# Adding the output projection to x straight from its bank, without ScalarE's copy

## The chip, the cores and the metric

The kernel runs on one core of a Trainium2 chip. The metric is the time on the device in microseconds (us): the median of several executions. The profile is one further execution, recorded by the hardware. TensorE (PE) multiplies matrices into eight banks of accumulators; VectorE (DVE) and ScalarE (ACT) can read these banks; GpSimd (POOL) here masks, divides and issues gathers and scatters; SyncE (SP) issues most of the transfers (DMA).

## The reference

One layer of a transformer over x of shape (8, 512, 256) in float32: attention, and then a mixture of experts.

```python
x = x + attn(layernorm(x))
# attn: qkv = x @ W_qkv + b_qkv; 16 heads of width 16, causal softmax of q k^T / 4
#       out = softmax(...) @ v;  return out @ W_out + b_out      (256 x 256)
x = x + ffn(layernorm(x))
# ffn: residual = x; xn = layernorm(x) * gamma + beta
#      probs = softmax(xn @ gate_w), 8 experts, the best 2 of each row with their shares
#      h = gelu(xn @ w1[e] + b1[e])  (256 -> 1024);  out_e = h @ w2[e] + b2[e]
#      return sum of the two out_e by share + residual
```

The change concerns `out @ W_out + b_out` and the `x +` in front of it.

## The kernel before

The kernel has three stages. In the **first** (about 140 us) the eight batches of 512 rows are normalised, turned and multiplied by `W_qkv`; q, k and v go to DRAM. The **attention** stage (to about 535 us) has 32 units, four heads of one batch each, so four units a batch. A unit is five combos; in each, TensorE computes scores in transposed form in two banks (`scores_T`, L657), whose exponentials ScalarE takes (L906, L903), and for a unit further on the scores in plain form (L629, masks L642), whose row maxima VectorE takes (`maxima`, L1236 to L1242). GpSimd masks the exponentials (L1699), TensorE weighs v by them (`weigh`, L701), ScalarE copies the result out (L926), and transfers through DRAM lay it out by heads; VectorE inverts the sums (L1249), GpSimd multiplies (`divide`, L1676). The **third** stage gathers rows by expert in 39 tiles and runs both layers of the experts (L776, L794), with gelu (L995) and the split of hidden values into two float16 parts (L1529, L1531), and scatters the results. Its first tiles run while the last batch is still on its way through the steps below.

Between attention and experts each batch b goes through a chain of its own, which is woven into the attention of the next batch:

- `load_again(b)` (SyncE, L1889) loads x of the batch again into `rows`, 512 KB. It waits until the batch before has given `rows` up.
- `out_proj(b, half)` (TensorE, L715 for the products in float32, L716 for the bias) makes 2 x 128 rows of the projection, 512 columns wide, in one bank.
- `copy_out(b, half)` (ScalarE, L959) copies the bank into `turned` in SBUF and frees the bank. `turned` also holds the turned rows of the batch before until `gate(b - 1)` (TensorE, L732) has read them.
- `add_out(b, half)` (VectorE, L1259) adds `turned` and `rows` into `x2`. It waits for the load of x (`x_again`) and until `x2` of the batch before has been stored (`rows_out`, L1977).
- then moments (L1266), variance, roots, shifts, scaling of rows on ScalarE (L935, L941), gamma and beta, the split of rows in two halves (L949, L1078), the turn of rows (L723, L931), the gate's product (L732) and its copy (`copy_gate`, L965), the choice of two experts and the places of rows.

**The order of the work is written down in advance.** `at(tick, stage, n)` puts each step at a tick of one table; every engine takes its own steps from the table in the order of ticks. A unit has 48 ticks and a batch 192. Ticks are places in an order and no times: an engine takes its next step when its semaphores allow, and never leaves one out. For batch b the base is the end of its four units plus 8 ticks (78 for the last batch); in that count the projection halves stand at 175 and 187, the copies at 181 and 193, the additions at 193 and 205, and the moments from 196 on. The gate of the batch before comes at 180 and its copy at 185.

**Banks.** Scores in transposed form and all the small products (top turns, projections, turned rows, gates, counts) take turns in banks 4, 5 and 6 in the order of the table; bank n's next user waits for the step that took out what the last one left (`TAKEN_BY`). For small products that was always ScalarE, counted by the semaphore `act_freed`; for scores it is the exponential (`exped`). So in batches 1 to 5 the order of uses is projection half 0, gate, then the two score halves of the first combo of a unit; the second of these has the bank that the projection had. In batch 0, without a gate, it is the projection's own second half.

Of the kernel before, what the change touches and what calls it, by code (L numbers as in the profile page):

```python
# [6 lines left out]
ALU = mybir.AluOpType  # L7
# [54 lines left out]
def build(nc, t):  # L62
# [54 lines left out]
    with ctx:  # L117
# [199 lines left out]
        def at(tick, stage, n):  # L317
            table_of.setdefault(tick, []).append((stage, n))
# [59 lines left out]
        for b in range(B):  # L378
# [3 lines left out]
            for half in range(2):  # L382
                at(base + 175 + 12 * half, "out_proj", (b, half))
                at(base + 181 + 12 * half, "copy_out", (b, half))
                at(base + 193 + 12 * half, "add_out", (b, half))
            for tt in range(TT):
# [52 lines left out]
        for j in range(-1, TILES):  # L439
# [10 lines left out]
            if j >= 0:  # L450
# [3 lines left out]
                if j + 2 < TILES:  # L454
# [8 lines left out]
        BANKS_A_UNIT = len(E_USES)  # L463
        TAKEN_BY = {"top_turn": "top_copy", "out_proj": "copy_out", "turn_x": "copy_x", "gate": "copy_gate",
                    "count": "copy_count"}
        uses, side, freed = [], {}, {"act_freed": 0, "exped": 0}
        for stage, n in timetable:
            if stage == "combo":
                for i in range(2):
                    freed["exped"] += 1  # L470
                    uses.append((("combo", n), ("combo", n), "exped", freed["exped"]))
            elif stage in TAKEN_BY:
                freed["act_freed"] += 1
# [356 lines left out]
        def scalar(act):  # L830
# [123 lines left out]

            def copy_out(b, half):
                w.wait_ge(sem("side_made"), side_made("out_proj", (b, half)))
                if b > 0:
                    w.wait_ge(sem("side_made"), side_made("gate", b - 1))
                act.copy(turned[:, half, :], side_bank("out_proj", (b, half))).then_inc(sem("act_freed"), 1)  # L959

            def copy_gate(b):
# [61 lines left out]
            for stage, n in timetable:  # L1023
# [6 lines left out]
                elif stage == "copy_o":  # L1030
                    copy_o(n)
                elif stage == "copy_out":
                    copy_out(*n)
                elif stage == "copy_gate":
# [37 lines left out]
        def vector(v):  # L1072
# [178 lines left out]
            def add_out(b, half):  # L1251
                w.wait_ge(sem("x_again"), 16 * (b + 1))
                w.wait_ge(*side_out("out_proj", (b, half)))
                if b > 0:
                    w.wait_ge(sem("rows_out"), 16 * b)
                else:
                    w.wait_ge(sem("v_store1"), 16 * (B // 2))
                own_x = slice(2 * half, 2 * half + 2)
                v.tensor_tensor(x2[:, own_x, :], turned[:, half, :].rearrange("p (s d) -> p s d", s=2), rows[:, own_x, :],  # L1259
                                ALU.add).then_inc(sem("out_added"), 1)  # L1260

# [756 lines left out]
```

## Time and profile before

| | |
|---|---|
| median of three runs | 972.66 us (967.0 to 973.46) |
| the profiled execution | 973.39 us, its span 971.6 us |
| TensorE busy | 844.1 us (87%), mean granted clock 0.927 of full speed |
| VectorE busy | 702.2 us (72%) |
| ScalarE busy | 572.8 us (59%) |
| GpSimd busy | 468.5 us (48%) |

The span runs from the first to the last instruction of the profiled execution. A row of the timeline has the start, the busy time, the engine, the line, the operation, what it writes and reads and how many instructions are merged in it; in square brackets stands how long the engine sat idle before it and what ended that. An idle time "issue" is one for which the profile shows no other engine or transfer as releaser. The lines of the program that load, store and add are seen under the names of the memory they lie in: `arena` and `weights` are SBUF, `banks` the accumulators. "SPq" is the issue of a transfer by SyncE; the transfer lands later. The granted clock of TensorE has two levels, 2.4 GHz (1.00) and 1.2 GHz (0.50); a mean between them is a mix over time.

### The profile page before, as it was taken

How to read it: one execution, taken by the hardware profiler on the slowest of the kernel's cores; microseconds unless marked ns; L12 is line 12 of the kernel's file. 1: busy time of each engine (PE TensorE's matmuls, PEld its weight loads, DVE VectorE, ACT ScalarE, POOL GpSimd, SP SyncE). 2: the span in 40 equal slices, each digit the busy share in tenths (PEclk: the TensorE clock that was granted, in tenths of full speed). 3: DMA queues.
4: the chain of work that ended last, by engine and by line, in shares of the span. 5: the costliest groups of instructions: out<-in, count | busy, mean ns of one | idle time of the engine just before them, and what ended most of it. 6: DMA issues, size and time to landing. Idle time of an engine off the chain costs nothing.

```text
span 971.6 us, 21008 instructions
## 1 busy us (share of the span) xinstructions
PE 844.1 (87%) x6760; PEld 555.8 (57%) x6760; DVE 702.2 (72%) x1566; ACT 572.8 (59%) x1048; POOL 468.5 (48%) x575
## 2 busy tenths in 40 slices
PE   4899988677797878787888797989989999999996
PEld 2555433233243424242434695869868888888875
DVE  6677888668669798979885585756756766656664
ACT  1767476546868787869776372545534445445453
POOL 4100033233535757657566556566566554554441
PEclk9999988779888979898997898989999999999998
DMA  8888667746767767576726884435535444444331
GB/s 202 253 274 270 235 190 195 194 113 170 206 195 204 184 188 198 163 200 179 203 75 208 169 145 69 58 79 98 79 55 79 79 78 73 76 76 83 52 73 23
DMA packets 185048, 139.40 MB, mean 143 GB/s; under 512 B 98065, under 2 KB 167569, under 8 KB 184817
## 3 DMA queue, kind: packets, MB, share of 16 engines
q1 hardware_dynamic: 153444, 95.16, 38.4%
q0 software_dynamic: 15776, 18.95, 12.3%
q10 hardware_dynamic: 15724, 23.95, 7.7%
q8 instruction: 61, 1.00, 0.4%
q14 instruction: 43, 0.34, 0.1%
HBM read 83.63 MB, written 44.80 MB: 132 GB/s over the span
## 4 chain that ended last, share of the span: by engine, by line
PE 54%; DVE 16%; DMA 13%; issue 5%; SPq 5%; ACT 3%; another core or an unknown queue 1%; POOL 1%; POOLq 0%; ACTq 0%; DVEq 0%
PE banks L776 18%; PE banks L794 18%; PE banks L598 5%; DMA weighed_values<-arena 3%; PE banks L715 3%; DVE arena L1239 3%; DMA inverse_sums<-arena 3%; DVE weights L1401 2%; PE banks L701 2%; PE banks L588 2%; PE banks L657 2%; SPq L1817 2%; DVE arena L1241 1%; SPq L1815 1%; DMA out<-arena 1%
## 5 line engine op out<-in xcount | busy, mean ns | idle before, releaser
L995 ACT ACTIVATE arena<-banks,arena 128x256 f32<-128x256 f32 (+1 forms) x312 | 152.4, 541 | 206.4 <-issue 95.7
L776 PE MATMUL banks<-arena,weights 128*128 128x256 f16 (+1 forms) x1872 | 210.9, 268 | 16.3 <-issue 15.7
L794 PE MATMUL banks<-weights,arena 128*128 x1704 | 198.2, 275 | 5.4 <-DVE arena L1531 3.1
L776 PEld LDWEIGHTS banks<-arena,weights 128*128 x1872 | 175.8, 99 | 45.5 <-issue 20.7
L1738 POOL DMA_INDIRECT out<-arena x71 | 117.0, 1648 | 159.1 <-DVE arena L1542 108.0
L794 PEld LDWEIGHTS banks<-weights,arena 128*128 128x128 f16 x1704 | 166.0, 99 | 31.1 <-issue 9.0
L657 PE MATMUL banks<-arena 64*128 64x128 f16 (+3 forms) x512 | 118.9, 330 | 32.8 <-ACT arena L931 9.3
L1529 DVE TENSOR_SCALAR arena<-arena 128x512 f16<-128x512 f32 (+1 forms) x156 | 76.9, 493 | 75.5 <-ACT arena L995 63.7
L629 PE MATMUL banks<-arena 62*128 62x384 f16 (+3 forms) x512 | 93.9, 326 | 32.5 <-DVE arena L1242 11.1
L1531 DVE SCALAR_TENSOR_TENSOR arena<-arena 128x512 f16<-128x512 f32 (+1 forms) x156 | 110.1, 706 | 5.6
L657 PEld LDWEIGHTS banks<-arena 64*128 64x128 f16 x512 | 38.0, 99 | 118.7 <-issue 36.3
L1239 DVE TENSOR_REDUCE arena<-banks 128x2 f32<-128x1024 f32 x64 | 77.8, 1216 | 31.0 <-PE banks L642 28.5
L906 ACT ACTIVATE arena<-banks,arena 128x512 f32<-128x512 f32 x128 | 81.3, 685 | 21.1 <-PE banks L657 20.7
L906 ACT ACTIVATE weights<-banks,arena 128x512 f32<-128x512 f32 x128 | 80.5, 685 | 12.4 <-PE banks L657 11.0
L1714 POOL DMA_INDIRECT arena<-token_rows,arena x71 | 75.2, 1060 | 21.1 <-issue 18.3
L1685 POOL DMA_INDIRECT slot_tokens<-arena x64 | 68.5, 1070 | 25.5 <-issue 16.3
L1241 DVE TENSOR_REDUCE arena<-banks 128x2 f32<-128x768 f32 x64 | 60.7, 949 | 22.7 <-PE banks L642 16.6
L1699 POOL TENSOR_SCALAR_AFFINE_SELECT weights<-weights 128x512 f32<-128x512 f32 (+1 forms) x80 | 45.2, 582 | 65.5 <-ACT weights L906 62.5
L1542 DVE SCALAR_TENSOR_TENSOR arena<-banks,arena 128x256 f32<-128x256 f32 x71 | 31.4, 480 | 62.1 <-PE banks L794 44.5
L1699 POOL TENSOR_SCALAR_AFFINE_SELECT arena<-arena 128x512 f32<-128x512 f32 (+1 forms) x80 | 49.1, 631 | 33.6 <-ACT arena L906 31.5
L701 PE MATMUL banks<-arena 128*32 128x256 f32 (+3 forms) x512 | 57.7, 530 | 4.8 <-ACT arena L926 2.4
L701 PE MATMUL banks<-weights 128*32 128x256 f32 (+3 forms) x512 | 57.7, 527 | 3.6 <-DMA weights<-v_rows 2.9
(199 smaller groups left out, 1259.9 us busy)
## 6 DMA issues: line engine op xcount, KB each, us to landing
weights<-in_L_ffn_w ACTq DMA_DIRECT2D x16, 1024.0 KB, 7.6
arena<-in_L_ffn_w SPq DMA_DIRECT2D x32, 512.0 KB
qk_parts<-weights SPq DMA_DIRECT2D x64, 128.0 KB
arena<-qk_parts SPq DMA_DIRECT2D x128, 64.0 KB, 3.5
weighed_values<-arena SPq DMA_DIRECT2D x32, 256.0 KB
token_rows<-arena SPq DMA_DIRECT2D x12, 512.0 KB, 4.3
arena<-qk_parts SPq DMA_DIRECT2D x128, 32.0 KB, 3.5
arena<-weighed_values SPq DMA_DIRECT2D x32, 128.0 KB
```

The lines of the kernel that those rows point to most:

```text
L629: pe.matmul(bank[:, to:to + (qt + 1) * P], q_st[u % 4][half, h, qt * P:qt * P + P], k_st[u % 4][half, h, 0:(qt + 1) * P], start=(to == 0), ...
L657: m = pe.matmul(turn_bank(number)[:, to:to + T - kt * P], k_st[u % 4][half, h, kt * P:kt * P + P], q_st[u % 4][half, h, kt * P:T], start=T ...
L701: m = pe.matmul(banks[32 * h:32 * h + 32, O_BANK, kt * P:T], v_and_ones(u, kt, h), p_T[u % 2][:, h, a:a + width], start=(kt == W_ORDER[0]) ...
L776: m = pe.matmul(bank[:, c * TILE:c * TILE + WIDTH[j]], w1[:, k, wp, f:f + P], xp[:, k, 0:WIDTH[j]], start=(i == 0), stop=(i == len(terms) ...
L794: m = pe.matmul(bank[:, c * D:(c + 1) * D], hp[:, f, c * P:(c + 1) * P], w2[:, f // (FC // 2), wp, f % (FC // 2), :], start=(f == 0 and i ...
L906: act.activation(p_T[u % 2][:, PAIR * h + j, PT_AT[kt]:PT_AT[kt] + T], bank, ACT.Exp, scale=EXP_SCALE).then_inc(sem("exped"), 1)
L995: m = act.activation(h_32[r % 2][:, c, 0:WIDTH[j]], banks[:, 1 + c2, c * TILE:c * TILE + WIDTH[j]], ACT.Gelu, bias=b1_now[j % 2][:, 2 * c2 ...
L1239: m = v.tensor_reduce(out[:, :, slot // 2, 3], pair, AX.X, ALU.max, negate=True)
L1529: m = own.mark(v.tensor_scalar(h_high[:, pair, width], h_32[r % 2][:, :, width], SCALE_H, None, ALU.mult))
L1531: v.scalar_tensor_tensor(h_low[:, pair, width], h_32[r % 2][:, :, width], SCALE_H, h_high[:, pair, width], ALU.mult, ALU.subtract).then_in ...
L1699: m = g.affine_select(out=area, in_=area, compare_op=ALU.is_ge, fill=0.0, base=0, pattern=pattern, channel_multiplier=-1)
L1738: g.indirect_dma_start(acc_dram[:, :], bass.IndirectOffsetOnAxis(slot_of(j, c), 0), y[j % 2][:, c, :], None, compute_op=ALU.add).then_inc( ...
```

## The change

The additions read the projection from its bank, and ScalarE's copy is left out. The addition frees the bank: `TAKEN_BY` no longer knows the projection, and its next user waits for the semaphore `out_added` (which the additions raised before as well, for the moments). Each addition also moves 12 ticks ahead, to where the copy stood, at 181 and 193. What it waits for besides, `x_again` and `rows_out`, stays. `turned` is used by turned rows alone.

```diff
--- before.py
+++ after.py
@@ -381,8 +381,7 @@
             base += 78 if b == B - 1 else 8
             for half in range(2):
                 at(base + 175 + 12 * half, "out_proj", (b, half))
-                at(base + 181 + 12 * half, "copy_out", (b, half))
-                at(base + 193 + 12 * half, "add_out", (b, half))
+                at(base + 181 + 12 * half, "add_out", (b, half))
             for tt in range(TT):
                 at(base + 196 + 3 * tt + 9 * (tt // 2), "moments", (b, tt))
             at(base + 218, "variance", b)
@@ -461,14 +460,17 @@
 
         TURNS, O_BANK = (4, 5, 6), 7
         BANKS_A_UNIT = len(E_USES)
-        TAKEN_BY = {"top_turn": "top_copy", "out_proj": "copy_out", "turn_x": "copy_x", "gate": "copy_gate",
-                    "count": "copy_count"}
-        uses, side, freed = [], {}, {"act_freed": 0, "exped": 0}
+        TAKEN_BY = {"top_turn": "top_copy", "turn_x": "copy_x", "gate": "copy_gate", "count": "copy_count"}
+        uses, side, freed = [], {}, {"act_freed": 0, "exped": 0, "out_added": 0}
         for stage, n in timetable:
             if stage == "combo":
                 for i in range(2):
                     freed["exped"] += 1
                     uses.append((("combo", n), ("combo", n), "exped", freed["exped"]))
+            elif stage == "out_proj":
+                freed["out_added"] += 1
+                side[(stage, n)] = (len(uses), len(side) + 1)
+                uses.append(((stage, n), ("add_out", n), "out_added", freed["out_added"]))
             elif stage in TAKEN_BY:
                 freed["act_freed"] += 1
                 side[(stage, n)] = (len(uses), len(side) + 1)
@@ -952,12 +954,6 @@
                 w.wait_ge(sem("gap"), b + 1)
                 act.activation(gap, gap, ACT.Exp).then_inc(sem("gate_exp"), 1)
 
-            def copy_out(b, half):
-                w.wait_ge(sem("side_made"), side_made("out_proj", (b, half)))
-                if b > 0:
-                    w.wait_ge(sem("side_made"), side_made("gate", b - 1))
-                act.copy(turned[:, half, :], side_bank("out_proj", (b, half))).then_inc(sem("act_freed"), 1)
-
             def copy_gate(b):
                 w.wait_ge(sem("side_made"), side_made("gate", b))
                 if b > 0:
@@ -1029,8 +1025,6 @@
                     top_in(n)
                 elif stage == "copy_o":
                     copy_o(n)
-                elif stage == "copy_out":
-                    copy_out(*n)
                 elif stage == "copy_gate":
                     copy_gate(n)
                 elif stage == "copy_count":
@@ -1250,14 +1244,14 @@
 
             def add_out(b, half):
                 w.wait_ge(sem("x_again"), 16 * (b + 1))
-                w.wait_ge(*side_out("out_proj", (b, half)))
+                w.wait_ge(sem("side_made"), side_made("out_proj", (b, half)))
                 if b > 0:
                     w.wait_ge(sem("rows_out"), 16 * b)
                 else:
                     w.wait_ge(sem("v_store1"), 16 * (B // 2))
                 own_x = slice(2 * half, 2 * half + 2)
-                v.tensor_tensor(x2[:, own_x, :], turned[:, half, :].rearrange("p (s d) -> p s d", s=2), rows[:, own_x, :],
-                                ALU.add).then_inc(sem("out_added"), 1)
+                v.tensor_tensor(x2[:, own_x, :], side_bank("out_proj", (b, half)).rearrange("p (s d) -> p s d", s=2),
+                                rows[:, own_x, :], ALU.add).then_inc(sem("out_added"), 1)
 
             norm_at = [0]
```

**VectorE, around the additions of batch 1** (L1239 to L1242 are maxima of scores, L1249 the inversion of sums, L1266 moments, L1401 the low part of a weight split). Before:

```order
L1239 TENSOR_REDUCE arena<-banks 128x2 [waits top_split,scored]
L1241 TENSOR_REDUCE arena<-banks 128x2 [waits scored]
L1242 TENSOR_REDUCE arena<-banks 128x2
L1249 RECIPROCAL arena<-arena 128x16 [waits inverse_kept1,o_moved1]
L1259 TENSOR_TENSOR arena<-arena 128x512 [waits rows_out,act_freed,x_again]
L1239 TENSOR_REDUCE arena<-banks 128x2 [waits scored]
L1266 BN_STATS arena<-arena 128x6 [waits out_added]
L1266 BN_STATS arena<-arena 128x6
L1241 TENSOR_REDUCE arena<-banks 128x2 [waits scored]
L1242 TENSOR_REDUCE arena<-banks 128x2
L1259 TENSOR_TENSOR arena<-arena 128x512 [waits act_freed]
```

With the change (the additions are L1253, the maxima L1233 to L1236, the inversion L1243, the moments L1260):

```order
L1233 TENSOR_REDUCE arena<-banks 128x2 [waits top_split,scored]
L1253 TENSOR_TENSOR arena<-banks,arena 128x512 [waits rows_out,side_made,x_again]
L1235 TENSOR_REDUCE arena<-banks 128x2 [waits scored]
L1236 TENSOR_REDUCE arena<-banks 128x2
L1243 RECIPROCAL arena<-arena 128x16 [waits inverse_kept1,o_moved1]
L1253 TENSOR_TENSOR arena<-banks,arena 128x512 [waits side_made]
L1233 TENSOR_REDUCE arena<-banks 128x2 [waits scored]
L1260 BN_STATS arena<-arena 128x6 [waits out_added]
L1260 BN_STATS arena<-arena 128x6
L1235 TENSOR_REDUCE arena<-banks 128x2 [waits scored]
L1236 TENSOR_REDUCE arena<-banks 128x2
```

The first addition, which stood behind a unit's second maximum and the inversion, now stands ahead of that maximum; the second, which stood behind the next two maxima and two moments, stands ahead of all of them. The first is the one that waits for `x_again` and `rows_out`.

**TensorE, from the gate of batch 0 (L732) to the second half of batch 1's projection (L715)**, where the banks of the first half are taken up again. Before:

```order
L732 MATMUL banks<-arena 128x8 x7
L657 MATMUL banks<-arena 128x512 [waits exped,top_in]
L629 MATMUL banks<-arena 128x384 [waits maxed]
L629 MATMUL banks<-arena 128x128
L629 MATMUL banks<-arena 128x384
L629 MATMUL banks<-arena 128x128
L657 MATMUL banks<-arena 128x512 [waits act_freed]
L642 MATMUL banks<-arena 128x256 x2
L715 MATMUL banks<-arena 128x256 [waits act_freed]
```

With the change:

```order
L734 MATMUL banks<-arena 128x8 x7
L659 MATMUL banks<-arena 128x512 [waits exped,top_in]
L631 MATMUL banks<-arena 128x384 [waits maxed]
L631 MATMUL banks<-arena 128x128
L631 MATMUL banks<-arena 128x384
L631 MATMUL banks<-arena 128x128
L659 MATMUL banks<-arena 128x512 [waits out_added]
L644 MATMUL banks<-arena 128x256 x2
L717 MATMUL banks<-arena 128x256 [waits act_freed]
```

No instruction moves. The second L657 of the combo (now L659), which takes the bank of the projection's first half, waits for `out_added`, VectorE's addition, where it waited for `act_freed`, ScalarE's copy.

**ScalarE, at the same place** (L926 copies weighed values, L965 the gate, L906 are exponentials, L888 the turned maxima). Before:

```order
L926 COPY arena<-banks 128x512 [waits o_kept,weighed]
L959 COPY arena<-banks 128x512 [waits side_made]
L965 COPY arena<-banks 128x32
L906 ACTIVATE weights<-banks,arena 128x512 [waits scored_T] x2
L959 COPY arena<-banks 128x512 [waits side_made]
L888 COPY arena<-banks 32x128 [waits top_in,side_made]
L906 ACTIVATE weights<-banks,arena 128x512 [waits scored_T] x2
```

With the change:

```order
L928 COPY arena<-banks 128x512 [waits o_kept,weighed]
L961 COPY arena<-banks 128x32 [waits side_made]
L908 ACTIVATE weights<-banks,arena 128x512 [waits scored_T] x2
L890 COPY arena<-banks 32x128 [waits top_in,side_made]
L908 ACTIVATE weights<-banks,arena 128x512 [waits scored_T] x2
```

Both copies L959 are gone; the gate's copy, now L961, has the wait that the first of them had.

## Rows read from the trace of the kernel before

**Rows 1.** The page's chain that ended last, shares of the span by engine

```profile
PE 54%; DVE 16%; DMA 13%; issue 5%; SPq 5%; ACT 3%; another core or an unknown queue 1%; POOL 1%; POOLq 0%; ACTq 0%; DVEq 0%
```

**Rows 2.** Busy us of PE, PEld, DVE, ACT, POOL by stretch; clock, DMA share, GB/s

```profile
268.00:279.00 11.00, 10.74 (x67) 7.35 (x69) 3.41 (x7) 4.82 (x11) 2.27 (x6) 0.84 0.81 231
279.00:320.00 41.00, 34.08 (x301) 13.99 (x302) 38.72 (x78) 35.60 (x63) 22.98 (x32) 0.88 0.67 191
...
330.00:372.00 42.00, 34.05 (x296) 12.75 (x292) 40.66 (x79) 36.37 (x62) 24.12 (x34) 0.88 0.64 181
```

**Rows 3.** Timeline behind batch 1's projection, VectorE and TensorE

```profile
281.97 0.68 DVE L1259 TENSOR_TENSOR arena<-arena 128x512 f32<-128x512 f32 x1
...
285.37 0.40 PE L629 MATMUL banks<-arena 62*128 62x384 f16 x4 [1.50 <-DVE arena L1236]
```

**Rows 4.** Timeline around batch 1's first projection half: VectorE, ScalarE, TensorE

```profile
268.17 1.23 DVE L1239 TENSOR_REDUCE arena<-banks 128x2 f32<-128x1024 f32 x1
273.76 0.96 DVE L1241 TENSOR_REDUCE arena<-banks 128x2 f32<-128x768 f32 x1 [4.37 <-PE banks L642]
...
272.16 0.58 ACT L959 COPY arena<-banks 128x512 f32<-128x512 f32 x1 [2.48 <-PE banks L732]
...
272.00 0.60 PE L629 MATMUL banks<-arena 62*128 62x384 f16 x4
```

**Rows 5.** Timeline of TensorE: the bank's next user, batches 0 to 5

```profile
219.39 1.10 PE L715 MATMUL banks<-arena 128*128 128x256 f32 x4
...
272.80 0.39 PE L657 MATMUL banks<-arena 64*128 64x512 f16 x1 [0.19 <-ACT arena L959]
...
323.71 0.39 PE L657 MATMUL banks<-arena 64*128 64x512 f16 x1 [0.20 <-ACT arena L959]
...
376.70 0.39 PE L657 MATMUL banks<-arena 64*128 64x512 f16 x1 [0.19 <-ACT arena L959]
...
430.85 0.39 PE L657 MATMUL banks<-arena 64*128 64x512 f16 x1 [0.19 <-ACT arena L959]
...
483.49 0.39 PE L657 MATMUL banks<-arena 64*128 64x512 f16 x1 [0.19 <-ACT arena L959]
```

**Rows 6.** By line: duration ns min/median/max, first and last start, forms

```profile
L959 ACT COPY arena<-banks x16: 567/585/587, 218.7 to 617.5; 128x512 f32<-128x512 f32 x16
...
L1259 DVE TENSOR_TENSOR arena<-arena x16: 628/682/695, 221.9 to 621.2; 128x512 f32<-128x512 f32 x16
...
L1165 DVE TENSOR_TENSOR arena<-banks,weights x8: 1052/1082/1111, 35.9 to 115.7; 128x512 f32<-128x512 f32 x8
```

**Rows 7.** Timeline of SyncE: issues of the reload of x, batches 0 to 5

```profile
215.07 0.48 SPq L1889 DMA_DIRECT2D arena<-in_L_attn_x  x1
...
267.51 0.57 SPq L1889 DMA_DIRECT2D arena<-in_L_attn_x  x1
...
319.37 0.49 SPq L1889 DMA_DIRECT2D arena<-in_L_attn_x  x1
...
371.00 0.53 SPq L1889 DMA_DIRECT2D arena<-in_L_attn_x  x1
...
426.23 0.55 SPq L1889 DMA_DIRECT2D arena<-in_L_attn_x  x1
...
478.37 0.54 SPq L1889 DMA_DIRECT2D arena<-in_L_attn_x  x1
```

**Rows 8.** Timeline of VectorE: first additions of batches 0 and 2

```profile
221.92 0.69 DVE L1259 TENSOR_TENSOR arena<-arena 128x512 f32<-128x512 f32 x1 [1.04 <-DMA arena<-in_L_attn_x]
...
326.46 0.69 DVE L1259 TENSOR_TENSOR arena<-arena 128x512 f32<-128x512 f32 x1 [0.56 <-issue]
```

**Rows 9.** The page's DMA issues: count, KB each, us to landing

```profile
token_rows<-arena SPq DMA_DIRECT2D x12, 512.0 KB, 4.3
...
weights<-in_L_attn_x ACTq DMA_DIRECT2D x7, 512.0 KB, 7.3
```

**Rows 10.** Timeline of TensorE: batch 0's first projection half

```profile
214.79 1.82 PE L715 MATMUL banks<-arena 128*128 128x256 f32 x4 [2.85 <-POOL arena L1676]
```

## The prediction

> **What bounds the kernel now.** I read first the chain of waits [rows 1]: TensorE carries half of it, VectorE a sixth, and transfers with SyncE's queue about a fifth (13% + 5%). ScalarE, whose work is taken away, carries 3%. So the question is not what 16 copies are worth but which wait they end.
>
> Then the busy time by stretch [rows 2], cut at the places where the output projection runs (once a batch, some 53 us apart). Two regimes alternate. In the 10 us of the projection and the gate TensorE is busy 10.7 of 11.0 us and VectorE only 3.4: TensorE bounds. In the 40 us between, VectorE is busy 38.7 of 41 and 40.7 of 42 us: VectorE bounds. The two additions of a batch are today one in each regime: the second one stands in the busy stretch, ahead of the split and the maximum for which TensorE then waits 1.50 us [rows 3].
>
> Last, the timeline around one projection (batch 1) [rows 4]. VectorE ends its maximum at 269.4 and idles 4.37 us. ScalarE waits 2.48 us for the gate's matmuls (its copy writes `turned`, which they read), and copies at 272.16. TensorE has the first half of the next unit's scores out at 272.60 and starts the second half (L657) at 272.80, released by that copy [rows 5]: this instruction takes the bank that the projection had. That restart is the place to watch; it comes once in each of batches 0 to 5 (in batch 0 it is the projection's own second half).
>
> **What leaves.** 16 copies of 0.585 us on ScalarE [rows 6], 9.4 us. Almost none lies on the path. The first of a batch ends the 0.20 us of TensorE's wait above; the gate's copy right behind needs the same matmuls, so ScalarE's 2.48 us wait stays. The second stands in the TensorE-bound stretch. Removing them gives 0.2 us in each of batches 1 to 5 if nothing else holds the bank, 1.0 in all.
>
> **What moves: the second addition.** It goes ahead of a maximum, into the stretch where VectorE idles, and leaves the VectorE-bound one. Its cover is the projection's second half on TensorE, which it waits for anyway. One addition frees 0.6 us (0.68, overlapped by its neighbours), in the six busy stretches that follow batches 0 to 5: **-3.6 us**.
>
> **What is new: the bank is held until x is there.** The first addition now frees the bank, and it waits for the reload of x (`x_again`), a 512 KB load, for `rows_out` and for its place on VectorE. VectorE is free early (269.4 in batch 1) and the projection done; x decides. Queued behind it on VectorE is the maximum of the running unit; TensorE waits for the bank, and ScalarE for TensorE's scores, so all three stop. In batch 0 the trace shows the landing: issued at 215.07 [rows 7], and VectorE, waiting, starts at 221.92 [rows 8], 6.85 us. Until now the copy had freed the bank at about 219.3 and TensorE went on at 219.39. For the other batches only bounds are seen. The same size takes 4.3 us in the median as a store, and 7.3 as a load in the opening [rows 9]; in batch 2 VectorE shows 0.56 us of unexplained idle ahead of the addition at 326.46 [rows 8], 7.1 us after the issue. I take 6.2, nearer to the loads than to the store. Restart = issue + 6.2 + 0.69 for the addition, against the restart now [rows 5, 7]:
> batch 1: 274.40 - 272.80 = 1.6; batch 2: 326.26 - 323.71 = 2.6; batch 3: 377.89 - 376.70 = 1.2; batch 4: 433.12 - 430.85 = 2.3; batch 5: 485.26 - 483.49 = 1.8; batch 0, measured landing: 222.61 - 219.39 = 3.2. Sum **+12.7 us**.
> With 4.3 us it is 3.2 for batch 0, 0.7 and 0.4 for batches 2 and 4, and a gain of about 0.2 in the other three: 3.7. With 6.85 it is 0.65 more in each of five: 15.9.
>
> **The clock.** In batch 0 the projection's first half, which follows 2.85 us of idle time, takes 1.82 us for four matmuls (1.2 GHz), the second 1.10 (2.4 GHz) [rows 5, 10]. With 3.2 us of idle time put ahead of the second half it may run at the lower level too: two groups, 1.5 us. I take half: **+0.8**.
>
> **The addition's price.** From SBUF 0.68 us; from a bank the nearest row is the addition of the value bias, same size but with a permuted output, 1.08 us [rows 6]. I take 0.69, since the access order stays plain; the upper end adds 0.4 in six places, 2.4 us.
> The Trainium skill ("VectorE: DVE Perf Modes", the TRN2 errata) gives VectorE 120 fixed cycles for a bank as source against 58 for SBUF at 0.96 GHz, which would be an estimated 0.06 us more for each addition, 0.4 in the sum; no row of this kernel has the same addition from both.
>
> **Absorption.** A stall is given back where the next waits are for transfers that run on meanwhile. About a fifth of the chain is such time [rows 1]; I take a fifth of 13.5: **-2.7**.
>
> **Batches 6 and 7** I cost at nothing. In 6 the next user of the bank is an expert matmul, which comes only after gathered rows have been turned by DMA. In 7 the first addition goes ahead of a split of hidden values; TensorE has queued expert work meanwhile, and x was loaded long before. Without that cover it would be one addition's wait each, 1 to 2 us.
>
> **Sum**: 12.7 + 0.8 - 3.6 - 2.7 = +7.2 on the profiled execution's 973.4, so 980.6. That execution lies 0.7 above the median of 972.66, so as a median **980**. In +12.7 the present restart is the reference, so the 1.0 us of the copies is counted only where x is early. For this kernel, whose three runs spread over 0.7%, less than 1% can't be told from no change; 1% slower is 982.4.
>
> **Rivals.**
> 1. *x lands early, and only the relief is left* (the other side). The place is the same wait; it decides where landing comes less than about 4.5 us after the issue (batch 1: 267.51 + 4.5 + 0.69 = 272.7, where TensorE is ready). For it: stores of the same size at 4.3 us; and the order can shift so that x is issued earlier against the projection. Against: batch 0. Price: -3.6 for the addition, -1.0 for the waits on the copy: 968 to 969; with batch 0's stall kept, 972. Chance 0.22.
> The Trainium skill ("DMA: Bandwidth & Descriptors", Anatomy of one DMA) fits a transfer as 2.0 us plus bytes over 436 GB/s, an estimated 3.2 us for 512 KB; by it x would be in time in all six batches and this rival would hold in full. By that fit, batch 0 would have landed at 218.3; the trace has 221.9, so it disagrees there.
> 2. *The stalls pull the clock down and nothing is given back.* TensorE idles 1 to 3 us in six places. Batches 1, 2 and 5 run the second half slowly already; 0, 3 and 4 would join them, 1.5 us each. With landing at 6.85: 15.9 + 4.5 - 3.6 = +16.8, or 990; with landing at 6.2 and no absorption, 987. For it: the row after 2.85 us of idle. Against: TensorE idles like this in many places and recovers. Chance 0.21.
> 3. *VectorE's relief counts more than once*, since the moments of rows and all that follows come earlier, and the stalls vanish: below 963. Nothing in the rows shows it. Chance 0.05.
> My forecast, 974 to 984, has 0.52.
>
> **Range and chances.** 968 to 990 takes in rival 1 and most of rival 2, and leaves out about 0.2. Slower by over 1% (above 982.4): rival 2 and the top of my own case, 0.13: 0.34. Faster by over 1%: rival 3 and a little of rival 1, 0.06. Within 1%: 0.60.
>
> **What the profile after would show.** Right: in each of batches 0 to 5 VectorE idles ahead of the first addition with the load of x as releaser, and TensorE's L659 (657 now), in batch 0 the projection's second half, waits for VectorE's addition, by 3 us in batch 0 and 1 to 3 us else. The second addition stands directly after the projection, and the busy stretches are shorter by 0.6 us each. ScalarE's busy time is 9.4 us less. The expert stage is as long as now. Wrong: no idle time ahead of the addition (rival 1), or a granted clock well under 0.92 with slow projection halves in batches 0, 3 and 4 (rival 2). If the 40 us stretches don't shorten, VectorE wasn't their bound; if they shorten by more than the addition, the chain of the rows' normalisation was.

## The result

The changed kernel takes 987.99 us, the median of 4 runs (986.84 to 988.99); the kernel before, on the same chip, 973.06 us (4 runs, 967.0 to 976.53). The ratio is 1.0154, 95% interval 1.0118 to 1.019: 1.5% slower. On another chip it was 1.0148 (1.0089 to 1.0206). The time lies in the forecast's range (968 to 990), above its likeliest case (974 to 984); "within 1%" was held likelier than "slower", and slower it is.

| | before | after |
|---|---|---|
| profiled execution, us | 973.39 | 986.84 |
| its span, us | 971.6 | 985.1 |
| mean granted clock | 0.927 | 0.928 |
| ScalarE busy, us | 572.8 | 564.6 |
| start of batch 0's projection, us | 214.79 | 209.46 |
| from there to the start of batch 6's, us | 311.44 | 329.29 |
| from there to the end, us | 445.37 | 446.35 |

**The chain of waits.** The page of the profile after, shares by engine and then by line; it answers to [rows 1].

```profile
PE 55%; DVE 14%; DMA 13%; SPq 6%; issue 6%; ACT 3%; another core or an unknown queue 1%; POOL 1%; POOLq 0%; ACTq 0%
PE banks L778 19%; PE banks L796 18%; PE banks L600 5%; DMA weighed_values<-arena 4%; PE banks L717 3%; DMA arena<-in_L_attn_x 3%; PE banks L703 2%; DVE arena L1233 2%; DMA inverse_sums<-arena 2%; PE banks L659 2%; DVE weights L1395 2%; DMA out<-arena 2%; PE banks L590 2%; SPq L1811 2%; SPq L1809 2%
```

By engine almost nothing moved. By line there is a new link: the load of x carries 3% of the span (2.6% unrounded, 25 us); before, it was no link of the chain. The shares by engine alone would not have shown it.

**The wait for x.** Timeline of SyncE (issues of x, batches 0 to 5), then of VectorE (first additions), answering to [rows 7, 8].

```profile
209.72 0.48 SPq L1883 DMA_DIRECT2D arena<-in_L_attn_x  x1
268.26 0.57 SPq L1883 DMA_DIRECT2D arena<-in_L_attn_x  x1
322.37 0.50 SPq L1883 DMA_DIRECT2D arena<-in_L_attn_x  x1
377.87 0.54 SPq L1883 DMA_DIRECT2D arena<-in_L_attn_x  x1
434.46 0.56 SPq L1883 DMA_DIRECT2D arena<-in_L_attn_x  x1
490.49 0.56 SPq L1883 DMA_DIRECT2D arena<-in_L_attn_x  x1
```

```profile
216.71 0.69 DVE L1253 TENSOR_TENSOR arena<-banks,arena 128x512 f32<-128x512 f32 x1 [7.95 <-DMA arena<-in_L_attn_x]
...
274.34 0.69 DVE L1253 TENSOR_TENSOR arena<-banks,arena 128x512 f32<-128x512 f32 x1 [4.71 <-DMA arena<-in_L_attn_x]
...
330.98 0.69 DVE L1253 TENSOR_TENSOR arena<-banks,arena 128x512 f32<-128x512 f32 x1 [6.75 <-DMA arena<-in_L_attn_x]
...
384.79 0.69 DVE L1253 TENSOR_TENSOR arena<-banks,arena 128x512 f32<-128x512 f32 x1 [3.17 <-DMA arena<-in_L_attn_x]
...
440.35 0.69 DVE L1253 TENSOR_TENSOR arena<-banks,arena 128x512 f32<-128x512 f32 x1 [3.09 <-DMA arena<-in_L_attn_x]
...
497.40 0.69 DVE L1253 TENSOR_TENSOR arena<-banks,arena 128x512 f32<-128x512 f32 x1 [3.44 <-DMA arena<-in_L_attn_x]
```

VectorE idles ahead of every one, with the load of x as releaser. The differences of the two lists are 6.99, 6.08, 8.61, 6.92, 5.89 and 6.91 us, 6.9 in the mean. Since VectorE waited each time, these are landings, for which before there was one row.

**TensorE behind it.** Timeline of TensorE, answering to [rows 5, 10]: batch 0's second projection half, and in batches 1 and 3 the projection and the two users of banks behind it.

```profile
217.45 2.07 PE L717 MATMUL banks<-arena 128*128 128x256 f32 x4 [3.48 <-DVE arena L1253]
...
268.42 1.10 PE L717 MATMUL banks<-arena 128*128 128x256 f32 x4
...
272.23 0.39 PE L659 MATMUL banks<-arena 64*128 64x512 f16 x1
...
275.08 0.60 PE L659 MATMUL banks<-arena 64*128 64x512 f16 x1 [2.25 <-DVE arena L1253]
...
385.54 0.39 PE L659 MATMUL banks<-arena 64*128 64x512 f16 x1 [2.27 <-DVE arena L1253]
386.08 1.53 PE L717 MATMUL banks<-arena 128*128 128x256 f32 x4
```

The user of the projection's bank starts 0.74 us after the addition (274.34, 275.08). The measure of the stall is the time from the projection's start to this restart: 4.61, 4.61, 4.58, 4.58, 4.58 us in batches 1 to 5 before, 6.66, 9.75, 6.66, 6.62, 6.59 after. With batch 0 (4.60, now 7.99) it is **+16.7 us**.

**The stretches.** Busy time of TensorE, its weight loads, VectorE, ScalarE and GpSimd, then clock, DMA share and GB/s, in batch 1's projection and gate and in the 40 us behind; it answers to the first two of [rows 2].

```profile
268.30:282.00 13.70, 11.39 (x63) 7.30 (x61) 4.16 (x7) 3.65 (x8) 2.27 (x6) 0.75 0.71 199
282.00:322.40 40.40, 31.96 (x301) 13.14 (x301) 37.73 (x77) 35.29 (x62) 21.96 (x32) 0.96 0.65 183
```

The projection's stretch was 11 us with TensorE busy 10.74; it is 13.7 with 11.39 busy, and the clock in it 0.75 in place of 0.84. In the other VectorE is still nearly always busy. How long the others are is better read from TensorE's starts than from cuts made by eye: from the restart to the next projection, batches 0 to 5 together, 283.9 us before and 285.0 after. That is 1.1 us more, though the second addition has left these stretches. But the same sum is 289.0 in a second trace of the kernel before and 288.7 in a second one of the change: it differs by 4 to 5 us between executions of one kernel, and can't show 3.6 us of relief. Whether VectorE was the bound of these stretches, as the prediction had it, is therefore not shown by them.

### The profile page after: what moved, and what is told of

It is laid out like the page before. It is cut to its first block, busy times and chain, and to the rows that moved or that the text cites. A ratio compares the mean times of both kernels' runs of the same rounds, so it can differ in the third digit from the quotient of the medians.

```text
span 985.1 us, 20991 instructions
## 1 busy us (share of the span) xinstructions
PE 841.8 (85%) x6760; PEld 555.6 (56%) x6760; DVE 700.9 (71%) x1566; ACT 564.6 (57%) x1032; POOL 466.4 (47%) x575
## 4 chain that ended last, share of the span: by engine, by line
PE 55%; DVE 14%; DMA 13%; SPq 6%; issue 6%; ACT 3%; another core or an unknown queue 1%; POOL 1%; POOLq 0%; ACTq 0%
PE banks L778 19%; PE banks L796 18%; PE banks L600 5%; DMA weighed_values<-arena 4%; PE banks L717 3%; DMA arena<-in_L_attn_x 3%; PE banks L703 2%; DVE arena L1233 2%; DMA inverse_sums<-arena 2%; PE banks L659 2%; DVE weights L1395 2%; DMA out<-arena 2%; PE banks L590 2%; SPq L1811 2%; SPq L1809 2%
## 5 line engine op out<-in xcount | busy, mean ns | idle before, releaser
L659 PE MATMUL banks<-arena 64*128 64x128 f16 (+3 forms) x512 | 118.0, 327 | 43.1 <-ACT arena L933 9.1
L659 PEld LDWEIGHTS banks<-arena 64*128 64x128 f16 x512 | 38.0, 98 | 125.9 <-issue 44.5
L1233 DVE TENSOR_REDUCE arena<-banks 128x2 f32<-128x1024 f32 x64 | 77.9, 1217 | 22.7 <-PE banks L644 22.4
L908 ACT ACTIVATE arena<-banks,arena 128x512 f32<-128x512 f32 x128 | 81.2, 685 | 16.8 <-PE banks L659 16.1
L1679 POOL DMA_INDIRECT slot_tokens<-arena x64 | 66.3, 1036 | 25.5 <-issue 16.6
L631 PEld LDWEIGHTS banks<-arena 62*128 62x128 f16 x512 | 28.9, 97 | 58.9 <-DMA arena<-qk_parts 16.6
```

What stands on the lines that cost most here:

```text
L631: pe.matmul(bank[:, to:to + (qt + 1) * P], q_st[u % 4][half, h, qt * P:qt * P + P], k_st[u % 4][half, h, 0:(qt + 1) * P], start=(to == 0), ...
L659: m = pe.matmul(turn_bank(number)[:, to:to + T - kt * P], k_st[u % 4][half, h, kt * P:kt * P + P], q_st[u % 4][half, h, kt * P:T], start=T ...
L908: act.activation(p_T[u % 2][:, PAIR * h + j, PT_AT[kt]:PT_AT[kt] + T], bank, ACT.Exp, scale=EXP_SCALE).then_inc(sem("exped"), 1)
L1233: m = v.tensor_reduce(out[:, :, slot // 2, 3], pair, AX.X, ALU.max, negate=True)
```

## The experiments

Ratios are against the kernel before on the same chip, with 95% intervals; the chips differ by up to 20 us, so times are compared within one chip only.

**No wait for x, the rest of the change in place.** The first line stands in ScalarE's scaling of rows, which now waits for the load; the others are in the addition.

```diff
+                w.wait_ge(sem("x_again"), 16 * (b + 1))
...
-                w.wait_ge(sem("x_again"), 16 * (b + 1))
+                w.wait_ge(sem("vectors_in"), 96)
...
-                                rows[:, own_x, :], ALU.add).then_inc(sem("out_added"), 1)
+                                gamma.unsqueeze(1).broadcast_to([P, 2, D]), ALU.add).then_inc(sem("out_added"), 1)
```

> The changed kernel, but the additions take gamma in place of x, so they never wait for the reload of x (the load still runs, and the scaling of rows waits for it); the output is therefore another. Theory (the bank is held until x has landed): the seven idle times of VectorE ahead of the first additions, 36.1 us in the profile of the change, and TensorE's 2 to 5 us in each of batches 0 to 5 are gone, and the time is at or a little under the kernel before: 965 to 974 us, against 988. Rival A (reading a bank, or VectorE's place in the order, is what costs): the time stays at 983 to 990. Rival B (half in the wait, half in a lower clock for other reasons): 975 to 982.

964.07 us against 975.54, ratio 0.9898 (0.9853 to 0.9944). Timeline of TensorE in batch 1:

```profile
262.21 1.10 PE L717 MATMUL banks<-arena 128*128 128x256 f32 x4
...
266.25 0.38 PE L659 MATMUL banks<-arena 64*128 64x512 f16 x1
266.79 1.03 PE L717 MATMUL banks<-arena 128*128 128x256 f32 x4
```

With x out of the way the change is a gain of 1%: the whole loss, and more, is the wait for x. The restart comes 4.0 us after the projection's start, in each of batches 1 to 5 (4.01 to 4.04), where the kernel before needs 4.6. The rows that are sent to the experts are others here, but from batch 6's projection to the end it takes 444.8 us against 445.4, so that is not where the gain lies.

**The additions early, the copies kept.** The kernel before, its additions at the change's place:

```diff
-                at(base + 193 + 12 * half, "add_out", (b, half))
+                at(base + 182 + 12 * half, "add_out", (b, half))
```

> The kernel before with its ScalarE copies, which free the bank; only the additions move ahead, to right behind the copies. VectorE waits for x as early as in the change, but no bank waits for it. Theory (the bank is what stops TensorE): TensorE's restart in batches 1 to 5 is 4.6 us after the start of the projection, as before, and VectorE's wait for x mostly falls into its idle time; the maxima come 0.5 to 1.5 us later in batches where x is late; 972 to 980 us. Rival (the blocked order of VectorE alone is enough, because the maxima behind the addition are needed): 984 to 990 us.

972.45 us, ratio 0.9937 (0.9908 to 0.9967). Batch 2, timelines of VectorE and of TensorE:

```profile
328.88 0.69 DVE L1259 TENSOR_TENSOR arena<-arena 128x512 f32<-128x512 f32 x1 [6.43 <-DMA arena<-in_L_attn_x]
```

```profile
324.81 0.39 PE L657 MATMUL banks<-arena 64*128 64x512 f16 x1 [0.19 <-ACT arena L959]
```

VectorE waits 6.43 us for x, as in the changed kernel, and TensorE has long gone on. The time is no longer for it than before: what costs in the change is not VectorE's wait but the bank that waits with it. The early place alone is a gain of about what the relief was put at (3.6 us): 3.1 between the medians, 6 by the ratio.

**Only the second half straight from its bank**, the first addition late as before, the second right behind it (12 ticks ahead of its old place).

```diff
-                at(base + 181 + 12 * half, "copy_out", (b, half))
-                at(base + 193 + 12 * half, "add_out", (b, half))
+                if half == 0:
+                    at(base + 181, "copy_out", (b, half))
+                at(base + 193, "add_out", (b, half))
...
+                made = turned[:, half, :] if half == 0 else side_bank("out_proj", (b, half))
```

> Half of the change: the first half of each projection is copied by ScalarE and added at its old place, the second half is added straight from its bank, right behind the first addition, when x has landed long ago. Theory: no wait for x that was not there before, TensorE restarts as before, and the second addition leaves VectorE's busy stretch (0.6 us in each of six): 968 to 973 us against 973 before. Rival (VectorE's relief is worth nothing, as the change's own stretches hardly shortened): 972 to 976. If reading the bank directly cost by itself: over 978.

971.42 us, ratio 0.9971 (0.9937 to 1.0006): no difference that can be measured. The second half's bank can wait for VectorE, since x is there by then. A mixture with the first half copied, the first addition early, the second direct, and x issued earlier did not add up either:

> The candidate for a better kernel than both: first half copied by ScalarE (the bank is free at once) and added right behind the copy, second half added straight from its bank, x loaded right behind the store of the rows. Theory: no bank waits for x, both additions lie in VectorE's idle time, eight copies are gone: 0.5 to 1% under the kernel before, 964 to 970 us if that gives 974. Rival (VectorE's wait for x ahead of a maximum eats the relief): within 0.3% of the kernel before.

972.6 us against 974.59, ratio 0.9985 (0.9954 to 1.0016). The 964 to 970 us expected were missed, and the time is the rival's; whether for its reason was not looked into.

**x issued earlier**, ahead of the store of the rows that SyncE issues in front of it:

```diff
-            at(base + 166, "load_again", b)
+            at(base + 162, "load_again", b)
```

> The change, with the reload of x 4 ticks earlier in SyncE's order, ahead of the store of the rows and of the two transfers of weighed values. Theory: the load is issued about 1 to 2 us earlier against the projection in batches 1 to 6, so TensorE's restart comes 1 to 2 us earlier in five batches; batch 0 unchanged: 978 to 984 us against 988. Rival (the landing is set by the traffic of the queue and not by the issue, or SyncE waits for the same thing anyway): 986 to 990.

977.28 us, ratio 0.9999 (0.9966 to 1.0032). Batch 1, timelines of SyncE and of VectorE:

```profile
263.58 0.40 SPq L1883 DMA_DIRECT2D arena<-in_L_attn_x  x1
264.03 0.50 SPq L1971 DMA_DIRECT2D token_rows<-arena  x1
```

```profile
269.86 0.69 DVE L1253 TENSOR_TENSOR arena<-banks,arena 128x512 f32<-128x512 f32 x1 [3.85 <-DMA token_rows<-arena]
```

The change's loss is gone, its gain not there. The addition now waits for the other transfer, the store of rows (`rows_out`), which went out behind x; the restarts are 6.60, 6.03, 4.02, 5.76 and 4.86 us after the projection's start. That is not all: in this profiled execution (981.67 us) it takes 89.1 us from batch 6's projection to batch 7's, where it takes 84.6 before and 84.1 in the change. Why was not found.

**x issued later**, and the change itself beside it on the same chip.

```diff
-            at(base + 166, "load_again", b)
+            at(base + 189, "load_again", b)
```

> The change, with the reload of x issued 23 ticks later, behind the eight transfers of the next unit's q and k: the suspected wait made longer, nothing else. Theory (TensorE restarts at landing plus one addition): the issue comes 4 to 5 us later against the projection in batches 1 to 5, and in batch 0 too, TensorE's restart by as much; six times 3.5 to 5 us, so 1007 to 1018 us. Rival (the stall is absorbed later by transfers that run on, a fifth as I took it): about 1003 to 1008. Rival (the wait for x isn't what costs): under 995.

> The changed kernel once more, word for word, as the reference for the other three on the same chip: 984 to 990 us, and 1.0 to 1.9% above the kernel before beside it. Should it lie within 0.5% of the kernel before here, the chip or the day would be the cause of the first difference, and not the change.

1014.46 us (ratio 1.0429, 1.0381 to 1.0477) and 988.88 us. Batch 1 with x late, timelines of SyncE, VectorE and TensorE:

```profile
279.72 0.42 SPq L1883 DMA_DIRECT2D arena<-in_L_attn_x  x1
```

```profile
284.27 0.69 DVE L1253 TENSOR_TENSOR arena<-banks,arena 128x512 f32<-128x512 f32 x1 [9.84 <-DMA arena<-in_L_attn_x]
```

```profile
285.02 0.61 PE L659 MATMUL banks<-arena 64*128 64x512 f16 x1 [7.38 <-DVE arena L1253]
```

Restarts from the projection's start, batches 1 to 5: 11.79, 10.73, 10.61, 11.16, 9.85, against 5.73, 6.94, 7.47, 8.01, 6.52 in the repeat of the change. With batch 0 (+2.9) the stall grew by 22.4 us. From batch 0's projection to batch 6's the profiled execution with x late takes 20.9 us more than the repeat (351.74 against 330.84), and the second projection halves run equally slowly in both (22.5 and 22.6 us for all six), so the clock has no part in it: 1.5 us of the 22.4 were given back. The profiled executions as a whole differ by 24.1 us, the medians by 25.6. A stall of the bank is paid nearly in full here.

The late load also landed sooner after its issue, 4.2 to 4.8 us in batches 0 to 5, where the same load took 5.6 to 8.0 in the repeat (the addition's start less the issue, VectorE idle ahead of each). The landing goes with where the load is issued, and no single figure holds for it.

**x early and in two loads**, right behind the store of rows; each addition waits for its own 256 KB.

```diff
-            at(base + 166, "load_again", b)
+            at(base + 164, "load_again", b)
...
-                w.wait_ge(sem("x_again"), 16 * (b + 1))
+                w.wait_ge(sem(f"x_again{half}"), 16 * (b + 1))
...
+                for half in range(2):
+                    own_x = slice(2 * half, 2 * half + 2)
+                    sp.dma_start(rows[:, own_x, :], x_rows(b)[:, own_x, :]).then_inc(sem(f"x_again{half}"), 16)
```

> The change, with the reload of x right behind the store of the rows and as two loads of 256 KB, each addition waiting for its own. Theory: the half lands 1 to 2 us sooner after its issue than the whole, and the issue comes 1 to 2 us earlier; of the 2 us stalls of batches 1 and 3 to 5 nothing is left, of those of batches 0 and 2 a part: 970 to 978 us. Rival (the order behind the store costs as much as it gives, as in the run with the load ahead of the store): 976 to 982.

965.87 us against 974.59 (ratio 0.9939, 0.9902 to 0.9977) and against 988.88 for the change: faster than both, and faster than the 970 to 978 us expected. The step has two parts, the earlier place and the two pieces; no run takes them apart. The same load in the kernel before, and with its copies and early additions, tells what each part is worth; all three ran on a third chip:

> The kernel before, with only the reload of x changed: right behind the store of the rows and in two halves. Theory: before, no bank waited for x, and VectorE waited for it only in batch 0 and shortly in batch 2, so nothing is gained: within 0.3% of the kernel before, 972 to 977 us. Rival (the load's order in SyncE's queue is itself what made the last version faster): 966 to 970.

> Copies of ScalarE kept, additions right behind them, reload of x early and in halves: the version with early halves less the one thing that the change is named after, the copy left out. Theory (most of the gain is VectorE's second addition moved into its idle time; the copies were worth 0.2 to 0.6 us in each of batches 1 to 5): 967 to 972 us, 1 to 4 us above the version without the copies. Rival (the copies are worth nothing): the same as that version; rival (all the gain is theirs): as the kernel before.

> The change with the reload of x early and in halves, once more, word for word, beside the two others on one chip: 0.4 to 1% under the kernel before, 965 to 970 us where that gives 974; below both others.

| on the third chip (before: 954.09 us) | us | ratio |
|---|---|---|
| load in early halves alone | 953.65 | 1.0009 (0.9974 to 1.0043) |
| and additions early, copies kept | 950.31 | 0.9985 (0.9946 to 1.0024) |
| and copies left out | 944.07 | 0.9908 (0.9879 to 0.9937) |

Leaving the copies out is worth 6.2 us between the last two lines; that is more than the 1 to 4 expected, and by the ratios the whole gain is theirs. Batch 1 with the copies, timeline of TensorE:

```profile
264.48 1.10 PE L715 MATMUL banks<-arena 128*128 128x256 f32 x4
...
268.28 0.39 PE L657 MATMUL banks<-arena 64*128 64x512 f16 x1
269.08 0.39 PE L657 MATMUL banks<-arena 64*128 64x512 f16 x1 [0.19 <-ACT arena L959]
269.63 1.92 PE L715 MATMUL banks<-arena 128*128 128x256 f32 x4
271.34 0.42 PE L716 MATMUL banks<-arena 128*128 128x256 bf16 x1
271.56 1.76 PE L715 MATMUL banks<-arena 128*128 128x256 f32 x4
...
274.42 0.23 PE L657 MATMUL banks<-arena 64*128 64x128 f16 x1
```

and without them:

```profile
265.61 1.10 PE L717 MATMUL banks<-arena 128*128 128x256 f32 x4
...
269.42 0.39 PE L659 MATMUL banks<-arena 64*128 64x512 f16 x1
269.65 0.38 PE L659 MATMUL banks<-arena 64*128 64x512 f16 x1
270.19 1.03 PE L717 MATMUL banks<-arena 128*128 128x256 f32 x4
...
271.16 1.03 PE L717 MATMUL banks<-arena 128*128 128x256 f32 x4
...
273.29 0.23 PE L659 MATMUL banks<-arena 64*128 64x128 f16 x1
```

The restart comes 0.80 us behind the instruction ahead of it (268.28, 269.08) with the copy, 0.23 without (269.42, 269.65). The row with the copy shows 0.19 us of idle time only, because matmuls of another line fill a part of the gap; the delay is 0.57. And the second projection half runs at 2.4 GHz (1.03 us for four matmuls) where it ran at 1.2 (1.92). From the restart to the third scores it takes 5.34, 5.26, 3.66, 3.65 and 4.33 us in batches 1 to 5 with the copies, 3.64 or 3.65 in all five without. 5 x 0.57 = 2.8 and 4.0 for the clock make 6.9, which looks like the 6.2 measured, but the same two traces don't bear this out. From batch 0's projection to batch 6's it takes 302.9 us with the copies and 301.2 without: 1.7 less (batch 0's own restart comes 1.1 us later without them, 5.51 against 4.44 us). From the restarts to the next projections, with the quicker second halves in them, it is 275.5 and 275.6 us, so the 4 us of the clock were lost again behind. Of the 6.5 us between the two spans 0.9 lie in the opening and 3.9 behind batch 6's projection. That leaving the copies out gains is measured; where the gain comes from is not shown.

**The kernel before, once more**, for a second trace.

> The kernel before, once more, for a second trace of it. In the first one batch 0's projection starts at 214.79 us and the first reload of x is issued at 215.07; with the change 209.46 and 209.72 (a repeat: 210.70 and 210.93), though the change touches nothing ahead of that. Theory A, that this is spread of the opening: the first issue lies anywhere from 208 to 215 here, and where it is early, the stretch from there to batch 6's issue (307.44 us in the first trace) is longer by about as much, up to 313. Theory B, that without the copies the opening ends earlier: first issue again at 213.5 to 215.5, stretch 306 to 309. In either case TensorE takes the bank of each projection's first half 4.58 to 4.61 us after the projection's start, and half or more of the second halves of batches 1 to 5 run at the lower clock.

One execution, 976.98 us; another one on the same chip took 969.82. Timelines of SyncE, and of TensorE in batch 2:

```profile
213.29 0.48 SPq L1889 DMA_DIRECT2D arena<-in_L_attn_x  x1
```

```profile
323.96 0.39 PE L657 MATMUL banks<-arena 64*128 64x512 f16 x1 [0.19 <-ACT arena L959]
324.51 1.03 PE L715 MATMUL banks<-arena 128*128 128x256 f32 x4
```

The restarts are the same, 4.58 to 4.61 us. From batch 0's projection to batch 6's it is 316.5 us (213.00 to 529.50), 5.1 more than in the first trace, so a part of the 17.9 us between the first two traces was chance. Batch 2's second half is fast here and was slow in the first trace, those of batches 3 and 4 the reverse. The first issue is late, 0.2 us ahead of theory B's bounds, and the stretch from it to batch 6's issue is longer than either theory had it, 313.68 us; neither holds in full. Batch 0's projection starts at 211.9 to 214.8 us in the five traces with all 16 copies and at 208.7 to 212.0 in the seven that have none: by some 3 us in the mean, and nearly apart. Why the opening should end earlier without copies that all come after it was not found; it stays open.

## Why the prediction was right, and where its terms were off

Between the two profiled executions (+13.5 us, predicted +7.2) the sum reads: opening -5.3, the six batches +17.9, the rest +1.0. The +17.9 are +16.7 of stall, 4.6 to 5.4 of clock (by two ways to count, in 4) and so some 4 given back. Against the second trace of the kernel before the batches take 12.8 us more, with the same stall (16.8) and 4.3 of clock, and so 8 given back. In the repeat of the change the stall is 14.5. That there is a stall of 14 to 17 us is firm; what the rest adds up from is known to some 3 us a term.

That the time fell into the range was in part luck. The prediction had no term for the opening, and what its terms missed in the six batches, some 11 us (6 against the second trace), would have put the execution above the range: without the opening's 5.3 us (3.5 against the second trace) it would have taken 990 to 992 us.

1. *Which wait ends what.* Right. The first addition waits for x, the bank waits with it, and TensorE's next user of the bank for the addition, in all six batches. The experiment without that wait, and the one in which VectorE waits and the bank doesn't, show both links.
2. *The stall, +12.7 predicted, +16.7 measured.* This is the term that was mis-sized. Landing was taken as 6.2 us from bounds of 4.3 and 7.3 [rows 9] and is 6.9 in the mean. The landings against 6.2 (batch 0: 6.85) add up to 3.6 of the 4.0 us that were missed, 2.4 of them in batch 2 alone, with 8.61 us. The one landing that the trace of before had measured, batch 0's 6.85 [rows 7, 8], was the best guess for all six; its sum, 15.9, stood in the prediction as the upper end of this term.
 The Trainium skill ("DMA: Bandwidth & Descriptors", Anatomy of one DMA) fits 2.0 us plus bytes over 436 GB/s for a transfer on GpSimd's software path, an estimated 3.2 us for 512 KB. The loads here go through SyncE's hardware queue among other traffic (0.71 of the DMA engines' time in batch 1's stretch) and took 5.89 to 8.61 us; by the fit rival 1 would have held, and the trace disagrees in all six.
3. *Absorption, a fifth, -2.7 predicted.* Not borne out. The share of the chain that is transfers was taken as the share of a stall that is given back. With x later, 1.5 of 22.4 us more of stall were given back in the six batches, where a fifth would be 4.5, and the medians show none. In the change itself absorption and relief can't be told apart: together they were put at 6.3, and the two traces of before leave 4 and 8. That the chain's transfers carry what the stalled engines make, and so start later with them, would explain a small share; it was not tested.
4. *The clock, +0.8 predicted, 4 to 5 us at the matmuls behind the restart.* Rival 2's mechanism was in force: in the changed kernel the second half runs wholly or for the most part at the lower level in all six batches. From restart to third scores, batches 1 to 5, it takes 27.4 us after, 24.0 and 25.2 in the two traces before; batch 0 adds 2.0 (its second half 4.21 us, before 2.19). By the second halves alone, from first to last matmul, it is 4.6. Whether these us reach the end is not shown: in the pair with and without copies above, 4 of them did not. Rival 2 had 990 with these landings; the stall and the slow halves in batches 0, 3 and 4 came out as it named them, and the opening took 5 us off. I gave it 0.21, too little: against it stood only that TensorE recovers elsewhere.
5. *The relief, -3.6 predicted.* Borne out within what the comparisons tell: 3.1 us by the early place alone on one chip, 3.3 on another (there with intervals that overlap). No stretch of a trace shows it by itself.
6. *The copies, 1.0 at most predicted, 6 measured where x is early.* The row was misread: 0.19 us of idle time ahead of the restart was taken for the delay. The delay is the distance between two starts, 0.80 against 0.23, which makes 2.8 us in place of 1.0. The other 3 us and more are not explained. In the changed kernel the term does not show, since x is later than the copy was.
7. *The addition's price.* 0.69 us from the bank, as taken; the 1.08 of [rows 6] was no guide. The line's row, count and min/median/max in ns:

```profile
L1253 DVE TENSOR_TENSOR arena<-banks,arena x16: 677/692/693, 216.7 to 630.5; 128x512 f32<-128x512 f32 x16
```

 Against 628/682/695 from SBUF that is 0.01 us in the median. The Trainium skill ("VectorE: DVE Perf Modes", the TRN2 errata) gives an estimated 0.06 us more; the trace shows a sixth of it.
8. *Batches 6 and 7 at nothing.* Right: VectorE waits 7.03 us for x in batch 6, and from that batch's projection to the end it takes 1.0 us more, from its reload of x 0.05 less (449.04 against 449.09).

## What to carry to other kernels

Before a PSUM bank is handed to a consumer that has a second operand, compare when that operand lands with when the bank (of the accumulators that TensorE writes) was freed until now: the bank is held until the later of the two, and a copy that looks idle may be what decouples them. If the operand can be issued a few us earlier, in pieces that each free their own bank, the copy can go; here this turned 1.5% slower into 0.6 to 0.9% faster. To price a wait, take the distance between starts of the same two instructions, not the idle time in a row; and before such local prices are added up to a measured difference, see whether the whole stretch shrank by as much.

## What the runs showed of the hardware

A 512 KB load issued by SyncE took 5.89 to 8.61 us to land in one execution, at the same place of successive batches, and 4.2 to 4.8 us in the run that issued it later in the order. The addition of 128 x 512 fp32 values with one operand in a PSUM bank takes VectorE 0.692 us in the median, 0.682 with both in SBUF. TensorE's second projection half ran at 2.4 GHz in batches 1 to 5 in all 15 cases of the three traces in which neither x nor a copy held the bank, and wholly or for the most part at 1.2 GHz in all five of the changed kernel, behind idle times of 2.19 to 5.33 us. With the first half's copy kept it was at either level from batch to batch and from execution to execution (in the run with only the second half direct, at 2.4 GHz in all five), behind the same 0.19 us of idle time, so that this idle time alone doesn't decide it; what does was not settled.
